# A decoder in four stages: a hardware loop and an earlier start in its channel attention, maxima kept in PSUM in its causal attention, constant matmuls in its workspace stage

## The reference

```
x = x + channel_attention(layernorm(x), ctx, ctx)    # 8 heads of 16 rows by 512
x = x + ternary_ffn(layernorm(x), w_up, w_down)      # Hadamard transform, ternary weights
x = x + causal_attention(layernorm(x), ctx, ctx)     # 16 heads of 32 channels, masked score -10000
x = x + workspace_ffn(x, ...)                        # 2 rounds: logits, top 4 tokens of each of 16 slots, write, project, mix
```

## Time and profile before

| what | value |
|---|---|
| time, median of 3 runs | 3771.95 us (3765.82 to 3773.39) |
| profiled execution | 3779.81 us, span 3777.9 us |
| mean granted TensorE clock | 0.987 |
| instructions | 73028 |
| busy in the span | PE 3537.5 us (94%), PEld 1778.8, DVE 2887.7 (76%), ACT 2554.2 (68%), POOL 1741.6 (46%) |
| channel attention | about 0 to 1580 us |
| ternary feed-forward | about 1610 to 2210 us |
| causal attention | about 2230 to 2900 us |
| workspace stage | about 2904 to 3778 us |

### The profile page before, as it was taken

How to read it: one execution, slowest core, us unless ns; L and a number is a source line. 1 busy time by engine, 2 the same in 40 slices (tenths; PEclk the granted TensorE clock), 3 DMA queues, 4 the chain that set the end, 5 groups by cost and what they waited for, 6 DMA issues and landing times. The chain is left out here.

```text
span 3777.9 us, 73028 instructions
## 1 busy us (share of the span) xinstructions
PE 3537.5 (94%) x25219; PEld 1778.8 (47%) x25219; DVE 2887.7 (76%) x4445; ACT 2554.2 (68%) x6417; POOL 1741.6 (46%) x2148
## 2 busy tenths in 40 slices
PE   6999999999999999889999979999997999999997
PEld 1222222222222222278788855555554666666664
DVE  7888888888888888768878858888886466574745
ACT  3777777777777777667777758878875454545454
POOL 5444444444444444077666624554553233342524
PEclk9999999999999999989999989999999999999999
DMA  7777677676677777433333313333452022120402
GB/s 123 123 124 124 120 122 123 118 123 121 120 124 124 124 124 138 125 99 124 116 118 115 117 61 101 108 107 103 129 177 86 1 68 68 41 95 4 132 1 79
DMA packets 344317, 392.11 MB, mean 104 GB/s; under 512 B 58640, under 2 KB 223120, under 8 KB 343952
## 3 DMA queue, kind: packets, MB, share of 16 engines
q1 hardware_dynamic: 316464, 352.03, 42.0%
q10 hardware_dynamic: 27488, 35.41, 3.7%
HBM read 200.65 MB, written 84.93 MB: 76 GB/s over the span
## 5 line engine op out<-in xcount | busy, mean ns | idle before, releaser
L385 DVE TENSOR_REDUCE a_neg_max<-a_max_ps 128x2 f32<-128x1024 f32 x1024 | 1209.9, 1220 | 199.6 <-PE a_max_ps L497 189.9
L529 ACT ACTIVATE a_P<-a_ring_ps 128x512 f32<-128x512 f32 x2048 | 1085.4, 603 | 407.7 <-PE a_ring_ps L477 398.5
L497 PE MATMUL a_max_ps<-a_K,a_Q 96*128 96x512 bf16 x2048 | 621.3, 385 | 32.6 <-DMA a_Q<-a_q_split 24.6
L477 PE MATMUL a_ring_ps<-a_Q,a_K 98*128 98x512 bf16 x2048 | 627.6, 384 | 14.4 <-DMA a_Q<-a_max_rows 10.1
L514 PE MATMUL a_pv_ps<-a_P,a_V 128*32 128x512 f32 x4096 | 545.7, 605 | 1.8 <-ACT a_out_sb L534 1.8
L477 PEld LDWEIGHTS a_ring_ps<-a_Q,a_K 98*128 98x128 bf16 x2048 | 157.9, 96 | 681.4 <-ACT a_P L529 497.8
L1334 ACT ACTIVATE c_P<-c_s_ps,c_bias 128x128 f32<-128x128 f32 x1024 | 368.1, 384 | 65.1 <-DVE c_bias L1170 64.8
L324 POOL TENSOR_SCALAR a_var_eps<-a_mean_var 128x1 f32<-128x1 f32 x64 | 12.3, 192 | 765.1 <-DVE a_mean_var L401 765.1
L497 PEld LDWEIGHTS a_max_ps<-a_K,a_Q 96*128 96x128 bf16 x2048 | 188.9, 98 | 220.8 <-DMA a_Q<-a_q_split 24.6
L1165 DVE TENSOR_REDUCE c_neg_max<-c_s_ps 128x4 f32<-128x512 f32 x256 | 175.7, 686 | 81.5 <-PE c_s_ps L1260 75.0
L1334 ACT ACTIVATION_READ_ACCUMULATOR c_P<-c_s_ps,c_bias 128x1 f32 x1024 | 228.4, 223 | 0.0
(11 more groups left out here) (271 smaller groups left out, 7267.7 us busy)
## 6 DMA issues: line engine op xcount, KB each, us to landing
a_K<-a_k_split SPq DMA_DIRECT2D x384, 128.0 KB, 7.1
a_Q<-a_q_split SPq DMA_DIRECT2D x378, 128.0 KB, 4.6
heads_out<-a_out_sb ACTq DMA_DIRECT2D x128, 256.0 KB, 4.6
w_first_in<-in_x_dram SPq DMA_DIRECT2D x112, 256.0 KB, 3.6
w_second_in<-in_ctx_dram SPq DMA_DIRECT2D x64, 256.0 KB, 4.9
w_third_in<-in_ctxT_dram SPq DMA_DIRECT2D x64, 256.0 KB, 5.0
x<-b_x SPq DMA_DIRECT2D x64, 256.0 KB, 2.1
c_x_in<-x SPq DMA_DIRECT2D x64, 256.0 KB, 3.6
```

What stands on the lines that cost most here:

```text
L385: dve.tensor_reduce(neg_max[:, p, 2 * u:2 * u + 2], max_ps[u % 2][:, :, :], AX.X, ALU.max, negate=True).then_inc(max_taken, 1)
L477: pe.matmul(ring(s, use_of(k))[:, :], K[i][:, h, n:n + 128], Q[i][:, h, :], start=True, stop=True).then_inc(scores_filled, 1)
L497: last = pe.matmul(max_ps[u % 2][:, j, :], Q[i][0:KROW, h, m:m + 128], K[i][0:KROW, h, :], start=True, stop=True)
L529: act.activation(P[p][k // NT][:, k % NT, :], ring(s, use_of(k))[:, :], ACT.Exp, scale=SCALE).then_inc(exp_done, 1)
```

## The change

Five edits, apart from names:

1. Channel attention: `run_steps` gets two more numbers. Steps up to `loop_from` and from `loop_to` on stay written out; between them a loop on the chip runs six steps per turn (19 turns on SP, POOL and VectorE, 20 on TensorE and ScalarE).
2. Its beginning: SP's step -2 issues the copies of batch 1 ahead of the load of batch 3; POOL splits the values of batch 0 in step -5 rather than in step -3.
3. Causal attention: the negated maxima are written to columns 256 to 259 of the scores' own PSUM bank, and the bias is made from there.
4. Workspace stage: in unit 0 TensorE gets 2, 11, 2, 5, 14 and 2 matmuls of a constant tile (`keep_busy`, 128x128 by 128x512 in bfloat16, into a bank that is free then). The tile is set by VectorE at the start of causal attention.
5. Workspace stage: the chosen weights are kept in `e_top` itself instead of in `w_raw`.

```diff
-def run_steps(eng, first, last, body):
-
-    for k in range(first, last + 1):
+def run_steps(eng, first, loop_from, loop_to, last, body):
+
+    assert (loop_to - loop_from) % 6 == 0
+    for k in range(first, loop_from):
         body(Step(0, k))
+    with eng.Fori(0, (loop_to - loop_from) // 6) as turn:
+        for k in range(6):
+            body(Step(turn, loop_from + k))
+    for k in range(loop_to, last + 1):
+        body(Step(0, k))
...
+def keep_busy(pe, bank, tile, n):
+
+    for _ in range(n):
+        pe.matmul(bank, tile[:, :], tile[:, :].unsqueeze(1).to_broadcast([128, 4, 128]), start=True, stop=True)
...
+                if s.k == -2:
+                    transfer_parts(s)
+                load_rows(s)
...
+                if s.k != -2:
+                    transfer_parts(s)
+            run_steps(sp, -8, 2, 116, 126, step)
...
+            def split_values(b, i, lap):
+                held.wait_ge(cT_loaded[i], lap * 16 + 16)
+                at_least(held, pv_done, (b - (NB - 1)) * (2 * NT))
+                pool.tensor_scalar(V[i][:, :, :, 0:D], cT_in[i][:, :].rearrange("p (t h d) -> p t h d", t=NT, d=D), 1.0, 0.0,
+                                   ALU.mult, ALU.add).then_inc(v_done, 1)
...
+                if s.half(3) == 0 and s.exists(3) and s.k != -3:
+                    split_values(s.batch(3), s.slot(3), s.lap(3))
+                if s.k == -5:
+                    split_values(0, 0, 0)
+            run_steps(pool, -6, 4, 118, 126, step)
...
+            run_steps(dve, -7, 1, 115, 125, step)
...
+            run_steps(pe, -2, 2, 122, 128, step)
...
+            run_steps(act, -1, 4, 124, 129, step)
...
-                        dve.tensor_reduce(neg_max[:, i, c * G:(c + 1) * G].rearrange("p (r g) -> p r g", r=2),
+                        dve.tensor_reduce(s_ps[:, c % 2, 0, 256:260].rearrange("p (r g) -> p r g", r=2),
                                           s_ps[:, c % 2, :, 0:256].rearrange("p r (g k) -> p r g k", g=2), AX.X, ALU.max, negate=True).then_inc(max_done, 1)
...
-                        dve.tensor_scalar(bias[:, i, c * G:(c + 1) * G], neg_max[:, i, c * G:(c + 1) * G], cols[:, 0:1], SCALE,
+                        dve.tensor_scalar(bias[:, i, c * G:(c + 1) * G], s_ps[:, c % 2, 0, 256:260], cols[:, 0:1], SCALE,
                                           ALU.min, ALU.mult).then_inc(bias_done, 1)
...
+            dve.memset(w.spare[:, :], 1.0).then_inc(w.spare_ready, 1)
...
                     last.then_inc(l_filled, 1)
+                    if f.k == 0:
+                        keep_busy(pe, xb_ps[1][:, :], w.spare, 2)
...
                     pe.transpose(ft[:, 0:128], lr[:, :, :].rearrange("p b s -> p (b s)"), identf[:, :]).then_inc(lg_filled, 1)
+                    if f.k == 0:
+                        keep_busy(pe, xb_ps[1][:, :], w.spare, 11)
...
                     pe.transpose(ft[:, 0:128], w_top[:, :], identf[:, :]).then_inc(wT_filled, 1)
+                    if f.k == 0:
+                        keep_busy(pe, xb_ps[1][:, :], w.spare, 2)
...
+                    if f.k == 0:
+                        keep_busy(pe, xb_ps[1][:, :], w.spare, 5)
                     for half in range(2):
                         ft = bank(pe, f, U_GT + half)
...
+                    if f.k == 0:
+                        keep_busy(pe, xb_ps[1][:, :], w.spare, 14)
                     ft = bank(pe, f, U_WST)
                     pe.wait_ge(ws_done, n + 1)
...
+                    if f.k == 0:
+                        keep_busy(pe, xb_ps[1][:, :], w.spare, 2)
                     pe.wait_ge(wsT_done, n + 1)
```

More of the change, by code:

```diff
@@ L247, in load_weights, with load_rows, transfer_parts @@
                 sp.dma_start(w_in[:, c, :].rearrange("p (k n) -> p k n", k=src.shape[1]), src).then_inc(w_loaded[c], 16)
+            def load_rows(s):
+                if s.half(8) == 0 and s.exists(8):
+                    b, i = s.batch(8), s.slot(8)
+                    at_least(held, q_split_done, b - (NB - 1))
+                    at_least(held, k_split_done, b - (NB - 1))
+                    at_least(held, v_done, b - (NB - 1))
+                    sp.dma_start(x_in[i][:, :], by_channel(x[b])).then_inc(x_loaded[i], 16)
+                    sp.dma_start(c_in[i][:, :], by_channel(ctx[b])).then_inc(c_loaded[i], 16)
+                    sp.dma_start(cT_in[i][:, :].rearrange("p (t c) -> p t c", t=NT), ctxT[b].rearrange("(t p) c -> p t c", p=128)).then_inc(cT_loaded[i], 16)
+            def transfer_parts(s):
+                if s.half(4) == 0 and s.exists(4):
+                    b, i = s.batch(4), s.slot(4)
+                    if s.k != -4:
+                        held.wait_ge(q_split_done, b + 1)
+                    held.wait_ge(k_split_done, b + 1)
+                    at_least(held, scores_filled, (b - (NB - 1)) * (2 * SCORES))
+                    if s.k != -4:
+                        for n, part in enumerate((0, 0, 1, 1, 0, 2)):
+                            sp.dma_start(Q[i][n * D:(n + 1) * D, :, :], q_split[:, i, part, :]).then_inc(Q_loaded[i], 16)
+                    for n, part in enumerate((0, 1, 0, 1, 2, 0)):
+                        sp.dma_start(K[i][n * D:(n + 1) * D, :, :], k_split[:, i, part, :]).then_inc(K_loaded[i], 16)
             def step(s):
@@ L1021, in causal_attention @@
         V = [sb(f"V{i}", [128, C], F32) for i in range(4)]
-        neg_max, bias = sb("neg_max", [128, 2, H], F32), sb("bias", [128, 2, H], F32)
+        bias = sb("bias", [128, 2, H], F32)
         P = sb("P", [128, 2, H, 128], F32)
@@ L1424, in workspace_ffn @@
         top, neg_top = sb("top", [128, 8]), sb("neg_top", [128, 1])
-        is_top, e_top, w_raw, w_top = sb("is_top", [128, 128]), sb("e_top", [128, 128]), sb("w_raw", [128, 128]), sb("w_top", [128, 128])
+        is_top, e_top, w_top = sb("is_top", [128, 128]), sb("e_top", [128, 128]), sb("w_top", [128, 128])
         w_sum, w_inv = sb("w_sum", [128, 1]), sb("w_inv", [128, 1])
@@ L1721, in step @@
                     dve.wait_ge(w_top_done, n * 2 + 1)
-                    dve.tensor_scalar(w_top[:, :], w_raw[:, :], w_inv[:, :], None, ALU.mult).then_inc(w_top_done, 1)
+                    dve.tensor_scalar(w_top[:, :], e_top[:, :], w_inv[:, :], None, ALU.mult).then_inc(w_top_done, 1)
                 if u.exists():
@@ L1790, in _ @@
             pe.wait_ge(const_ready, 10)
+            pe.wait_ge(w.spare_ready, 1)
             def step(f, u, after):
```

21 lines of the change are left out of this document (2 added, 19 removed).

## The result

The kernel after takes 3723.78 us (median of 4, 3720.39 to 3729.88) where the kernel before took 3769.44 on the same chip (3765.82 to 3773.39): ratio 0.988, interval 0.9863 to 0.9898. On a second chip the same kernel took 3726.19 against 3764.01, ratio 0.9898 (0.9882 to 0.9915), 37.8 us less. The profiled execution has a span of 3723.3 us.

What follows compares the result with a forecast made beforehand. The prediction took TensorE's work alone to bound channel attention. Beginning -8.5, maxima in PSUM -12.5, fillers -3.5 and loop +4 gave -20.5 us, from a median of 3771.95 to 3751.5; range 3741 to 3780.

Steps and rivals of the forecast that it cites:

- TensorE's own work: Channel attention: the 11.90 us step was TensorE's work, with only 0.19 us of waits, before the transpose of the maxima.
- 1.6 us to spare: Channel attention: VectorE was said to have 1.6 us free per step, from its busy time over the stage.
- -1 at most: Channel-attention loop, lower bound: at most 1 us gained, since TensorE's 33 us idle was for exponentials and copies left unchanged.
- +4: Channel-attention loop: 4 us slower, from 0.03 us in each of 128 steps in the hand-over from score to exponential.
- A: Rival, chance 0.16: the loop's back edge stops VectorE, and ScalarE with it; +63 in place of +4, 3810 us.
- the bound of +63: Channel-attention loop, upper bound: each of 19 turns fetches code by a copy, 4.9 us less 1.6 to spare.
- B: Rival, chance 0.17: waits on registers hand over more slowly, 0.1 us more per channel-attention step, 12.8 in all; 3760.3 us.
- C: Rival, chance 0.08: maxima in PSUM free nothing in causal attention and a long bias stays; 3764 us.
- D: Rival, chance 0.11: the beginning gains only its first stop and the fillers gain what they cost; 3758.8 us.
- Forecast -8.5: Beginning of channel attention: earlier copies of batch 1 remove TensorE's early stops and warm it sooner; 8.5 us less.
- Forecast -12.5: Causal attention, maxima in PSUM: 60 batches at 0.20 us plus 0.5 for the last one; 12.5 us less.
- Forecast -3.5: Workspace stage, first unit: constant matmuls keep the clock full, -1.8 - 1.8 - 0.6 + 0.7; 3.5 us less.

Runs made afterwards that it cites:

- e3: Kernel before, written out, with TensorE's waits for exponentials and for maxima parts exchanged before the transpose of turned maxima: 3756.80 us, ratio 0.9980.
- e11: Kernel after with VectorE's channel-attention steps written out, the other four engines looped: 3717.83 us, ratio 0.9881 to the kernel before.
- e1: Kernel before with only the loop of all five engines added: 3747.89 us, ratio 0.9957.
- e9: Kernel before, written out, with waits exchanged on TensorE (before the turned maxima) and ScalarE (scores ahead of value products): 3749.34 us, ratio 0.9963.
- e4: Kernel before with the loop on TensorE alone, the other four engines written out: 3744.05 us, ratio 0.9943.
- e7: Kernel before with only the maxima of causal attention moved to PSUM: 3754.88 us, ratio 0.9971.
- e8: Kernel after without the 36 constant matmuls: 3729.90 us, ratio 0.9907 to the kernel before.
- e2: Kernel before with only the new beginning of channel attention, every step written out: 3759.22 us, ratio 0.9983.
- e5: Kernel before, unchanged, run again for a second profile: 3766.17 us, ratio 1.0003.
- e6: Kernel after, unchanged, run again on a second chip: 3726.19 us, ratio 0.9898 to the kernel before.

## Why the prediction was wrong

**What bounds the kernel.** That only TensorE's time counts in channel attention was right. That the step is "TensorE's own work" was not. The period was taken from one pair of transposes; the 124 steps between the earlier trace rows and the last one have a mean of 12.01, and the 0.11 between the two numbers, 14 us in the stage, was never asked about. The 0.19 in front of L486 was read as part of the work; 0.09 of it went when two waits were exchanged (e3). Nor does VectorE have 1.6 us to spare at every point of a step: that is its mean idle time, and a reduction 0.15 to 0.35 us later already lengthens the step (e11).

**The loop: the step that failed.** "-1 at most ... I take +4", with a ground for excluding a gain: "TensorE idles 33 us in the stage, for exponentials and copies that the loop doesn't change". It changes both. And the +4 itself rests on 0.03 us per step in a hand-over, for which no row was shown; the runs have that hand-over 0.06 us faster. Alone the loop measures 16.2 us less (e1): 124 x 0.14 = 17 us from the shorter step (e9 has the same step without a loop), plus some 10 from the code copies that are no longer made (e4), less 8 to 10 for VectorE's loop (e11). The difference to +4 is 20 us, against a miss of 25 in the first measurement and 17 in the second.

**Rivals.** A: no turn shows a stall of TensorE; with the loop on TensorE alone the 113 steps have 0.8 us beyond the usual one. The backward branch takes 0.21 us in TensorE's own queue and 0.04 to 0.07 in the others', and matmuls run on under it without a gap. Nor does a turn fetch code again, as the bound of +63 had it: with 6 copies of q8 left in the stage there is not one per turn. What VectorE's loop costs, 0.5 us a turn, comes in three steps and not at the branch. The Trainium skill (Runtime: NRT & Kernel Launch, "Instruction fetch mechanics") says that the cost of fetching straight-line code is mostly hidden, and that kernels prefer full unrolling, since a branch to code that is not held must fetch it first. On the first these runs say otherwise: the straight-line fetch costs 10 us, through the copies it delays. On the second, no run here shows a branch to code that is not held; unrolling was the slower choice for TensorE and the faster one for VectorE. B had the right place and the wrong sign: the hand-over to the weight load of L486 became faster, by 0.06, and the hand-over to ScalarE too. Only VectorE's became slower. C fell (e7). D had two halves: that the fillers gain nothing fell (e8), but that the beginning gains 4.7 and not 8.5 is nearer to what e2 measured, 5.0 or 6.4 less (2.6 to 10.5).

**The beginning.** Forecast -8.5, measured 6.3 less by starts. Mechanism and order of events as described; the size was off because a second stop of 0.5 to 3.8 us and the stretch at half the clock behind it, which differ from execution to execution, were taken from one profile (e5). In the first pair of profiles the start is 12.5 us earlier, in the mean of all 6.3: that the forecast of 8.5 lies between the two is luck.

**Maxima in PSUM.** Forecast -12.5, measured 11 to 16 by the stage, 10.9 by the ratio. The late batches were put at 0.20 each, 0.32 more at the low end, and cost 0.5 to 1.5. The Trainium skill (VectorE: DVE Perf Modes, "Why PSUM operands drop a tier") says that a PSUM operand keeps an operation out of the mode that needs both SBUF read ports. The trace agrees with what the prediction drew from it: 222 ns for all 219, also under POOL's addition.

**Fillers.** Forecast -3.5, measured 2.7 to 3.7. The 14 fit (0.40 us of waiting is left behind them); the 5 push the transposes to 2870.95, up to 1.1 us, where 0.7 was costed.

With e1, e2 and e7 and the difference of e6 and e8 the parts sum to 16.2 + 6.4 + 10.9 + 3.7 = 37.2, against 37.8 measured for all. The first three are uncertain by 4 to 5 us each, so that the sum comes so close is partly luck. Of the 45.7 of the first chip some 8 us stay unassigned; its interval reaches down to 38.4, and 5 of the 8 lie in the kernel before, whose median is 3769.44 of four runs there against 3764.0 to 3764.3 of 60 runs on the other chips.

## What to carry to other kernels

Compare the mean period over a whole stage with the shortest one before calling a step pure work, and lay the starts of the instruction copies beside the long steps. Where an engine waits for two semaphores, ask for the one that comes last first in the source, so that the working instruction carries it: that was worth 15 us here for two exchanged lines. Here the loop paid on the engine with the most instructions (e4), and cost on VectorE, whose hand-overs are on the path (e11); try it for each engine by itself. And a wait that no view names may only have become too short for it.

## What the runs showed of the hardware

TensorE's code comes in 16 KB copies, one in about two steps (64 in the stage before, 6 after), which the page lists with the other DMA packets. While one is under way, issues on other engines take up to 2.69 us instead of 0.62 (SP, L270) and 1.99 instead of 1.16 (ScalarE, two issues of L549); how the copy slows them is not shown. A wait in an instruction of its own adds about 60 ns to a hand-over on TensorE (113 against 50) and on ScalarE (486 against 427). Register arithmetic between the waits of VectorE's loop puts its reductions 0.15 to 0.35 us later (e11).
